# Shared-expert tiles that take their turned tokens and their split weights from the stage ahead

## What is computed

```python
x = L0_attn_x                                   # 8 x 512 x 256
xn = _layernorm(x)
x = x + _L0_attn_ref(xn, ...) + _L0_ffn_ref(xn, ...)
...
def _L0_ffn_ref(x, gate_w, gate_b, w1, b1, w3, b3, w2, b2, sw1, ...):
    scores = softmax(xf @ gate_w.T)             # 4096 tokens, 8 experts, the best 2 are used
    h = silu((xf @ w1 + b1) * (xf @ w3 + b3))   # each expert: 256 -> 352 -> 256
    y = sum over the two chosen experts of score * (h @ w2 + b2)
    z = _expert(xf, sw1, sb1, sw3, sb3, sw2, sb2)    # the shared expert: every token
    return y + z
```

## Time and profile before

| | us |
|---|---|
| three timed runs | 1232.79, 1238.09, 1236.97 (median 1236.97) |
| the profiled execution | 1237.58 |
| its span in the trace | 1235.8 |
| attention stage, in the span | 0 to 460 |
| experts stage, in the span | 463.6 to 845 |
| PE, DVE, ACT, POOL busy | 1124, 914, 682, 530 |
| mean granted clock of PE | 0.977 |

### The profile page before, as it was taken

One profiled execution on the slowest core, in us unless ns is written; L12 is line 12 of the kernel. 1 busy time (PEld: TensorE's weight loads), 2 busy tenths in 40 slices (PEclk: granted clock), 3 DMA queues, 4 the chain that ended last, 5 costly groups with the idle time before them and its releaser, 6 DMA issues. The chain is left out here.

```text
span 1235.8 us, 26934 instructions
## 1 busy us (share of the span) xinstructions
PE 1124.0 (91%) x8964; PEld 751.5 (61%) x8965; DVE 914.1 (74%) x2224; ACT 682.2 (55%) x1478; POOL 529.9 (43%) x751
## 2 busy tenths in 40 slices
PE   4789999999999966998999999997999999999998
PEld 2345555555555435887999888883555555546555
DVE  4778898888887826885756667674877977977866
ACT  2256565665556544665656666655554654664553
POOL 5343333424333228833444443332635546447314
PEclk9689999999999997999999999998999999999999
DMA  4437524445234106656232453442231241332302
GB/s 137 82 72 215 108 45 95 95 78 102 45 79 87 18 35 190 192 161 197 76 126 81 123 163 122 121 141 69 81 126 41 97 129 42 102 94 72 107 8 97
DMA packets 98276, 125.17 MB, mean 101 GB/s; under 512 B 14480, under 2 KB 87888, under 8 KB 97168
## 3 DMA queue, kind: packets, MB, share of 16 engines
q1 hardware_dynamic: 87184, 105.07, 31.9%
q0 software_dynamic: 6912, 18.88, 5.5%
q10 hardware_dynamic: 4096, 0.14, 0.2%
HBM read 84.70 MB, written 39.19 MB: 100 GB/s over the span
## 5 line engine op out<-in xcount | busy, mean ns | idle before, releaser
L479 ACT ACTIVATE p<-bank 128x384 f32<-128x384 f32 (+1 forms) x384 | 191.5, 530 | 186.0 <-PE bank L855 119.6
L688 DVE TENSOR_REDUCE neg_max<-bank 128x1 f16<-128x384 f32 (+3 forms) x352 | 219.6, 640 | 65.0 <-PE bank L843 62.2
L397 POOL TENSOR_SCALAR_AFFINE_SELECT p<-p 128x256 f32<-128x256 f32 x256 | 103.6, 409 | 245.4 <-ACT p L479 244.7
L121 PE MATMUL xbank<-gT_hi,w_hi 128*128 128x256 f16 (+1 forms) x636 | 175.0, 275 | 15.3 <-DVE w_lo L1448 6.0
L122 PE MATMUL xbank<-gT_lo,w_hi 128*128 128x256 f16 (+1 forms) x636 | 174.7, 275 | 0.0
L123 PE MATMUL xbank<-gT_hi,w_lo 128*128 128x256 f16 (+1 forms) x636 | 174.6, 274 | 0.0
L840 PE MATMUL bank<-k_stack,q_stack 96*128 96x384 f16 (+3 forms) x512 | 133.5, 313 | 20.1 <-DVE neg_max L688 12.6
L1382 ACT ACTIVATE a<-xbank,b 128x256 f32<-128x256 f32 x159 | 74.3, 468 | 65.9 <-PE xbank L123 62.4
L1293 POOL DMA_INDIRECT fetched<-xn_dram,token_now x80 | 81.4, 1017 | 42.9 <-POOL token_now L1289 30.7
L1934 POOL TENSOR_TENSOR up_lo<-up_sq,up_hi 128x512 f16<-128x512 f32 x32 | 43.2, 1378 | 126.6 <-ACT up_hi L1991 126.6
L1467 DVE SCALAR_TENSOR_TENSOR prod<-xbank,b,a 128x256 f32<-128x256 f32 x159 | 73.8, 476 | 31.4 <-ACT a L1382 23.7
(11 more groups left out here) (304 smaller groups left out, 3065.5 us busy)
## 6 DMA issues: line engine op xcount, KB each, us to landing
w_bc<-wT_dram SPq DMA_DIRECT2D x8, 2048.0 KB, 8.3
y_routed_dram<-y SPq DMA_DIRECT2D x37, 256.0 KB, 2.1
w<-in_w SPq DMA_DIRECT2D x11, 704.0 KB, 6.8
pack<-in_pack SPq DMA_DIRECT2D x12, 342.0 KB, 4.0
xr<-in_x SPq DMA_DIRECT2D x8, 512.0 KB, 7.3
xn_dram<-xn SPq DMA_DIRECT2D x8, 512.0 KB, 3.1
qk_hi_dram<-qk_hi SPq DMA_DIRECT2D x16, 256.0 KB, 2.8
qk_lo_dram<-qk_lo SPq DMA_DIRECT2D x16, 256.0 KB, 2.6
```

The costliest lines, as they stand in the source:

```text
L121: pe.matmul(out, hi_a(c), hi_b(c), start=first and x == 0, stop=False)
L397: pool.affine_select(out=diagonal, in_=diagonal, pattern=[[0, 2], [1, P]], compare_op=ALU.is_ge, fill=0.0, base=0, channel_multiplier=-1). ...
L479: act.activation(p32[:, s // GH % 2, s % GH, cols], s_bank[n][:, 0:cols.stop - cols.start], ACT.Exp).then_inc(p_exp.sem, 1)
L688: dve.tensor_reduce(neg_max[:, g % 2, 0:GH * TT].rearrange("p (h t) -> p h t", t=TT)[:, heads[0]:heads[-1] + 1, j], a_bank[c % 2][:, 0:len ...
```

## The change

- The attention stage stores `xT_hi` and `xT_lo` of each batch to a new DRAM tensor `xnT` (two DMAs a batch, 256 KB each).
- The fifteen shared tiles that read rows in order load from it into `turned`, two buffers, by one DMA of 256 KB (`load_turned`). Their transposes, `gT_hi` and `gT_lo` are gone. Only routed tiles and the gathered one are still turned in the stage.
- `load_shared` brings the shared expert's weights into buffers that the last batch has left free, and ACT and DVE split them at units 31, 33, 36, 38 and 33, 35, 38, 40 of that batch. The halves, two turned tiles and the biases are held over the barrier in `Carried`, which takes the place of `wqkv32`, `wout32` and `q32`.
- The end of the attention stage no longer waits for the last `x1` store; SP waits for it later, in `last`.
- POOL's 8 `in_column` move to DVE: eight instead of seven in each of tiles 0 to 7.
- SP loads the first routed expert's weights in tile 1 and the second's in tile 3 (before: tile 0 and 1). The four loads of `tail_rows` (1 MB at the end of the head) are gone.

```diff
+PLACED_BY_DVE = 64
+PLACED_A_TILE = 8
...
+            def store_xT(b):
+                sp.wait_ge(xT_lo_s.sem, xT_lo_s.at(b))
+                for k, of in enumerate((xT_hi, xT_lo)):
+                    sp.dma_start(dram["xnT"][b][:, k], of[:, :, :]).then_inc(xT_stored.sem, 16)
+
+            def load_shared():
...
+                sp.dma_start(w13_32[0], w["w13"][0][0:P, :]).then_inc(shared_in_loaded.sem, 16)
...
+                for n in range(2):
+                    sp.dma_start(carried.turned[:, n], turned_tile(dram["xnT"], n)).then_inc(turned_loaded[n].sem, 16)
...
+            store_xT(0)
             for half in range(2):
                 store_hi(0, half)
...
                 if b + 1 < NB:
+                    store_xT(b + 1)
                     store_hi(b + 1, 0)
...
+                if b + 1 == NB:
+                    sp.wait_ge(xT_stored.sem, xT_stored.at(0))
+                    load_shared()
                 if b >= 1:
                     store_x1(b - 1)
...
-            sp.wait_ge(x1_stored.sem, x1_stored.at(NB - 1))
+            sp.wait_ge(x1_stored.sem, x1_stored.at(NB - 2))
+            sp.wait_ge(xT_stored.sem, xT_stored.at(NB - 1))
...
+                    elif at - 28 in AT_SHARED:
+                        split_shared(AT_SHARED.index(at - 28))
...
+            def load_turned(n, tile, read):
+
+                sp.wait_ge(gu_psum.sem, gu_psum.at(read))
+                sp.dma_start(turned[:, n % 2], turned_tile(dram["xnT"], tile)).then_inc(turned_loaded[n % 2].sem, 16)
...
-                if stage == HEAD:
-                    load_x(i + AHEAD)
                 load_pack(i)
+                load_turned(i + 2, i + 2 + (i + 2) // HEAD_TILES, i)
...
             def prologue():
                 find_slots()
-                x_part(0)
-                for c in range(DC):
-                    split_in(0, 0, c, 0)
-                split_out(0, 0, 0)
...
             def tile(i, u, before, stage, to_split=None):
-                pe.wait_ge(gT_lo_s.sem, gT_lo_s.at(i))
-                gate_up(i, u, 0)
-                gate_up(i, u, 1)
-                if has_next(stage):
-                    x_transposes(i + 1, stage == HEAD or is_int(i, HEAD_TILES - AHEAD), stage + 1 if stage in range(TAIL_TILES) else 0)
-                gate_up(i, u, 2)
+                n = shared_place(i, stage)
+                if n is None:
+                    pe.wait_ge(gT_lo_s.sem, gT_lo_s.at(i - HEAD_TILES))
+                else:
+                    pe.wait_ge(turned_loaded[n % 2].sem, turned_loaded[n % 2].at(n // 2))
+                gate_up(i, u, 0, n)
+                gate_up(i, u, 1, n)
+                if next_routed(i, stage):
+                    x_transposes(i + 1)
+                gate_up(i, u, 2, n)
```

More of the change, by code:

```diff
@@ L95, with __init__, sb, turned_tile @@
 AT_MAX = {0: (0, 1), 1: (2, 3)}
+AT_SHARED = (3, 5, 8, 10)
 AT_VALUES, AT_COPY, AT_TURN, AT_DIVIDE = {5: (0, 3), 8: (1, 2)}, 11, 1, 2
+class Carried:
+    def __init__(self, nc, ctx):
+        def sb(name, shape, dt=F32):
+            return ctx.enter_context(nc.sbuf_tensor(name, shape, dt))
+        self.first = sb("shared_in", [P, 2 * DC * 3 * D], F16)
+        self.second = sb("shared_out", [P, 2 * len(HT) * D], F16)
+        self.turned = sb("turned", [P, 2, 2, DC, ETOK], F16)
+        self.bias = sb("shared_b13", [P, 2 * len(HT)])
+        self.turned_loaded = [Signal(nc, ctx, f"turned_loaded{u}", 16) for u in range(2)]
+        self.x1_stored = Signal(nc, ctx, "x1_stored", 16)
+        n = DC * 2 * H0
+        self.w13_hi, self.w13_lo = (self.first[:, k * n:(k + 1) * n].rearrange("p (c n) -> p c n", c=DC) for k in range(2))
+        n = len(HT) * D
+        self.w2_hi, self.w2_lo = (self.second[:, k * n:(k + 1) * n].rearrange("p (m n) -> p m n", m=len(HT)) for k in range(2))
+def turned_tile(t, tile):
+    per = S // ETOK
+    return t[tile // per][:, :, :, tile % per * ETOK:(tile % per + 1) * ETOK]
 def is_int(i, n):
```

219 lines of the change are left out of this document (117 added, 102 removed).

## The result

| | before | changed |
|---|---|---|
| median of 7 runs each, us | 1236.97 | 1229.04 |
| lowest to highest, us | 1232.79 to 1243.53 | 1224.86 to 1231.65 |
| profiled execution: its time, and the span in it | 1237.6, 1235.8 | 1228.5, 1226.7 |
| ratio to before, 95% interval | | 0.9941 (0.9917 to 0.9965) |

The change gains 7.9 us; 18 were forecast. The sign is right, the size is not: 1229 lies outside the range of 1212 to 1228.

What follows compares the result with a forecast made beforehand. It took PE's idle boundary, then nearly full PE and DVE with DVE pacing tiles 0 to 7, as the bound. Gains 16.7, 0.4, 1.5, 2.3 less losses 0.7, 1.3 gave -18.9 from 1237.6: 1219 us, range 1212 to 1228.

Steps and rivals of the forecast that it cites:

- Step 6: Head up to the table: table starts at 518.3 instead of 535.01, gain 16.7 us, with better cover for turned rows.
- The tail: Tail: no wait for gT_lo (1.05 us) and three tiles without transposes (0.43 each); gain 2.3 us, between 0.6 and 2.8.
- Steps 3 and 4: Head tile on DVE: first prod to h_lo 2.91 us, y 0.66, eight placements 2.0, pack 0.78; 6.35 in all.
- The second rival: Front and attention stage: clock falls, splits cost in full, start and placements cost more; 5.1 us slower, 1224 us; chance 0.26.
- Steps 1, 2 and 7: Head: block starts 2.4 us earlier without the barrier's wait, first prod at 467.0, POOL done by about 512.5.
- tiles 9 and 10: Head's last tiles, without placements: tile 9 loses its transposes on PE, gain 0.4 us; tile 10 still turns routed rows.
- The first routed expert: Behind the head: tail_rows load gone, SP's loads move up, PE's 3.49 us wait shrinks; gain 1.5 us, between 0 and 3.5.
- The attention stage: Attention stage: loss 0.7 us at the start from stores ahead of qk, 1.3 from ACT's splits in the last batch.
- the third rival: Attention stage: xT stores ahead of qk delay the stacks in seven more batches, 22.8 us in all; 1241.5 us; chance 0.04.
- The fourth rival: Head: turned rows in 512 B pieces cost PE 1.5 us for each of nine loads, 13.5 us; 1232 us; chance 0.07.

Runs made afterwards that it cites:

- e1: Changed kernel with the first routed expert's biases and weights asked for in tile 1 ahead of the store of tile 0; 1226.9 us, 0.991 of the kernel before.
- e9: Changed kernel with the first routed expert's biases and weights asked for in tile 2, right behind tile 4's turned rows; 1250.1 us, 0.989 of the kernel before.
- e3: Changed kernel with the tail's turned rows asked for ahead of the store of the tile before; 1225.9 us, 0.990 of the kernel before.
- e14: Changed kernel with three SP orders: first expert's weights in tile 0, tail's turned rows first, x2 read late; 1246.2 us, 0.987 of the kernel before.
- e4: Changed kernel with the wait for the last x1 store put back at the attention stage's end; 1232.1 us, 0.996 of the kernel before.
- e8: As e5, with the 512 KB x2 read moved into the tail behind its first tile's store; 1249.8 us, 0.985 of the kernel before.
- e11: As e14, with ACT's four splits moved to units 13, 16, 22 and 25 of the last batch; 1250.0 us, 0.988 of the kernel before.
- e6: As e5, with GpSimd's 64 comparisons replaced by one clearing, so the table is wrong; 1261.0 us in one execution.
- e5: Changed kernel with the first expert's weights asked for in tile 0 and the tail's turned rows ahead of the store; 1253.6 us, 0.988 of the kernel before.
- e13: The changed kernel measured again on the third chip; 1255.2 us, 0.993 of the kernel before.

## Why the forecast was wrong, by its own steps

**Step 6, the missed one.** "... a turned tile is asked for when gate_up of tile i ends and needed at tile i+2 ... and the 1 MB weight loads stand behind it in tiles 1 and 3." The second half is true and beside the point. The weights stand behind the rows of tiles 3 and 5, and therefore ahead of the rows of tiles 4 and 6; I had asked what is in front of two requests and never what is behind the bulk. Tile 6 had the time for it, tile 4 had not. PE's 5.00 us and DVE's 3.03 us, and the matmuls at half speed behind them, make tiles 3 and 4 take 9.7 and 8.4 us on DVE (their first prods and the next tile's stand at 488.10, 497.81 and 506.23) against 6.5: about 5 us. The case of the kernel before was no guide: there the rows were asked for at another point of the list. The trace shows the order of issue and when each load is used. The Trainium skill, DMA: Bandwidth & Descriptors, section Queues, rings and completion order, says that each DMA engine takes the descriptors of one queue in ring order. By that rule, read against SP's list, the risk could have been foreseen, though not its size; e1 and e9 agree with it.

**The tail, the other.** I credited 2.3 us for a wait that goes and for three tiles' transposes. The wait did go (the tail's first y is 11.7 us ahead, 0.8 more than the fourth routed one), and the transposes are worth 1.0 in e3. What I left out is that the rows, which used to be there since the end of the head (the 1 MB of tail_rows that the first expert's term took off), are now asked for two tiles ahead on a list on which a store that waits for y stands first: 2.66 us of wait, and 1.6 in which 17 matmuls stand 0.21 us apart instead of 0.11. The two terms were two sides of one move, and I booked only the gain.

**Steps 3 and 4, sizes.** The chain of 2.91 us was 2.83, y and pack exact. Eight placements beside GpSimd take 2.23 us, not 2.0; alone 1.76. The two errors cancel: in e14 the seven tiles from the y of tile 0 (479.31) to that of tile 7 (523.88) take 44.6 us, five of 6.50 beside GpSimd and two of 6.03 behind it, forecast 7 x 6.35 = 44.45. Tile 0 took 6.82 us from prod to prod instead of 5.41: ACT's table load lay on the path with all of its 1.28 us and the last bias ahead of it, ready only at 468.99, with some 0.3 (I had put 0.5 for both), and the placements took 0.3 more than forecast. The second rival had named these, the falling clock included (PE was idle for 2.16 us over the boundary, and the matmuls of tile 0 take 0.42 us from 463.9 to 466.9).

**Steps 1, 2 and 7, right.** The barrier is worth 2.42 us (e4). The first prod came at 468.22, 1.1 of it the attention stage's, so 467.1 against 467.0. GpSimd was done at 509.9, forecast 512.5. Tile 8 took the 1.4 us before the table, and tiles 9 and 10 brought 0.6, forecast 0.4 (the difference goes from 9.3 to 9.9).

**The first routed expert.** 1.0 us (the wait fell from 3.49 to 2.50), forecast 1.5. The range given for it, up to the whole wait, was right in kind: e8 wins 3.4 by taking away the other thing that stood ahead, the read of x2.

**The attention stage.** At the start the first x1 is 0.55 us late (135.86 for 135.31), and the loss has gone by the fifth; 0.7 forecast. The splits cost 1.1, forecast 1.3. No batch is held up by the stores of xT in the changed kernel, so the third rival did not occur.

**The fourth rival** named the wait for turned rows and priced it at 1.5 us for each of nine loads; its 1232 is the case nearest to what came. Its mechanism was another: one load of nine waited, and one of the tail. Its 0.07 was too little for a load that had never been in this place.

In sum: 5.4 us up to the table (6.3 in the head, less 0.9 by which the attention stage did better than charged), 0.5 at the first expert and 5.1 in the tail (2.3 expected, 2.8 lost from the fourth routed y to the tail's last), less 0.2 that tiles 9 and 10 brought beyond the forecast and 1.0 that the changed execution took off behind the tail. That is the 9.8 between -18.9 and -9.1.

## What to carry to other kernels

When a load is moved, write down the whole list of its queue from the last bulk transfer to the moved one, with the time at which each entry is released: it is what stands behind the bulk, or behind a store that is released late, and is needed soon, that waits. Changing such an order was worth 3.4 to 4.7 us here, in three places; in the tail it was 4.6 on the first chip and 0.9 on the third. A preload that a change takes away is a gain where it stood and a new load with its own place in the queue where it was used; book both. And I would no longer take an engine's idle time before an instruction for slack when its releaser may move with it (argued from e11, not tested).

## What the runs showed of the hardware

**A long GpSimd instruction held VectorE for all of its length.** In e6, first GpSimd, then VectorE:

```profile
468.49 7.00 POOL L1395 MEMSET in_lane<- 128x8192 f16 x1 [4.90 <-DVE tail_at L1667]
```

```profile
468.54 6.97 DVE L1607 COPY slot<-pos 128x8 int32<-128x8 int32 x1
468.61 6.91 DVE L1608 COPY wk<-route_weights 128x8 f32<-128x8 f32 x1
468.69 6.84 DVE L1534 SCALAR_TENSOR_TENSOR prod<-xbank,shared_b,a 128x256 f32<-128x256 f32 x3
```

A copy of 8 columns, 0.17 us otherwise, takes 6.97 and all three end with the clearing; PE then waited 6.77 us for prod. The Trainium skill, SBUF — State Buffer, section Who interferes with whom, calls the port pair that the two engines share an exclusive lock: against a VectorE instruction in a 2-port mode, which it says a copy can be, whoever comes first has it for the whole instruction and the other fully blocks. The trace agrees for the first copy, which starts 0.05 us behind the clearing; whether the second copy and the prods were held themselves or only stood behind the first, the rows don't tell. Beside the 64 short comparisons (0.6 us each) a tile took 0.47 us longer than without them (e5 and e6), 0.06 for each placement.

**The same program took 2.2 to 2.5% longer on two of the three chips** (1267.0 and 1263.7 us against 1236.7). From 850 to 1150 us PE was busy for 283 us in the changed kernel as first measured and for 267 in e13, the same kernel, at nearly the same clock (1.00 and 0.99).
